# Attention inside a one-core AdaLN block: score products woven between the next head's key and query products, with two buffers for queries and keys

## The reference

```
x1  = ln(x) * (1 + scale1) + shift1
q, k, v = x1 @ qkv_w + qkv_b            # 16 heads of 128
p   = softmax(q k^T / sqrt(128))        # 128 x 128 for each sequence and head
x   = x + gate1 * ((p v) @ out_w + out_b)
x2  = ln(x) * (1 + scale2) + shift2
x   = x + gate2 * (gelu(x2 @ ffn_w1 + ffn_b1) @ ffn_w2 + ffn_b2)
out = x0 + ternary feed-forward of x (relu squared, rms norm)
```

## Time and profile before

| | us |
|---|---|
| median of 3 runs | 390.71 |
| lowest, highest | 390.7, 392.43 |
| profiled execution, span from first to last instruction | 391.2 |
| PE busy in it | 367.8 |
| DVE, ACT, POOL busy | 288.0, 237.0, 129.7 |
| mean granted PE clock | 0.980 |

### The profile page before, as it was taken

The page is one execution under the profiler, slowest core; times in us unless marked ns, Lnnn a source line. Parts: engine busy times, 40 slices in busy tenths (PEclk is TensorE's granted clock), DMA queues, the critical chain, the costliest instruction groups (busy, mean ns, idle before and its releaser), DMA issues. The chain is left out here.

```text
span 391.2 us, 6260 instructions
## 1 busy us (share of the span) xinstructions
PE 367.8 (94%) x2096; PEld 319.5 (82%) x2096; DVE 288.0 (74%) x486; ACT 237.0 (61%) x582; POOL 129.7 (33%) x111
## 2 busy tenths in 40 slices
PE   2899999999999999999999999999889899996975
PEld 2789888888888888888888898889778787885855
DVE  5775569768776976866887667689988638797793
ACT  1464576665666566656676566775687358573751
POOL 1522224321542232272323144335423300162451
PEclk9999999999999999999999999999999999998995
DMA  7913031000303100030200012010000000000002
GB/s 231 358 61 108 1 109 54 2 0 3 108 0 107 54 0 0 0 107 29 78 0 0 0 26 83 0 55 1 2 0 1 2 0 2 0 1 2 8 19 80
DMA packets 11778, 16.53 MB, mean 42 GB/s; under 512 B 672, under 2 KB 7920, under 8 KB 11760
## 3 DMA queue, kind: packets, MB, share of 16 engines
q1 hardware_dynamic: 11760, 16.30, 12.6%
HBM read 15.25 MB, written 1.05 MB: 42 GB/s over the span
## 5 line engine op out<-in xcount | busy, mean ns | idle before, releaser
L345 POOL TENSOR_TENSOR prob<-prob,rinv 128x512 f32<-128x512 f32 x32 | 33.4, 1043 | 152.4 <-DVE rinv L788 152.4
L980 PE MATMUL bank<-x_hi,wqk_hi 128*128 128x512 f32 x128 | 54.4, 425 | 0.0
L982 PE MATMUL bank<-x_hi,wqk_lo 128*128 128x512 f32 x128 | 51.3, 401 | 0.0
L981 PE MATMUL bank<-x_lo,wqk_hi 128*128 128x512 f32 x128 | 51.1, 399 | 0.0
L706 DVE TENSOR_TENSOR v_lo<-bank,v_hi 128x512 fp32r<-128x512 f32 x30 | 20.7, 691 | 39.2 <-ACT v_hi L427 39.2
L493 ACT ACTIVATE prob<-bank,nbias 128x128 f32<-128x128 f32 x128 | 45.1, 370 | 4.1 <-DVE nbias L782 4.1
L427 ACT ACTIVATE p_split<-bank 128x512 fp32r<-128x512 f32 x32 | 19.1, 598 | 35.4 <-PE bank L1014 35.4
L461 ACT ACTIVATE o_hi<-pv_pair,bias 128x512 fp32r<-128x512 f32 x31 | 21.3, 688 | 24.3 <-PE pv_pair L1029 24.3
L982 PE MATMUL bank<-k_hi,q_lo 128*128 128x128 f32 x128 | 35.4, 276 | 0.0
L417 POOL TENSOR_TENSOR raw_qk<-raw_qk 128x512 f32<-128x512 f32 x13 | 18.4, 1415 | 50.7 <-ACT raw_qk L622 50.4
L981 PE MATMUL bank<-k_lo,q_hi 128*128 128x128 f32 x128 | 35.2, 275 | 0.0
(11 more groups left out here) (206 smaller groups left out, 1086.9 us busy)
## 6 DMA issues: line engine op xcount, KB each, us to landing
raw_qk<-in_L_cond_qkv_w_dram SPq DMA_DIRECT2D x8, 512.0 KB, 4.9
raw_v<-in_L_cond_qkv_w_dram SPq DMA_DIRECT2D x4, 512.0 KB, 3.8
raw_o<-in_L_cond_out_w_dram SPq DMA_DIRECT2D x4, 512.0 KB, 3.6
xt<-in_x_dram SPq DMA_DIRECT2D x2, 512.0 KB, 5.0
xr<-in_L_cond_ada_w_dram SPq DMA_DIRECT2D x1, 1024.0 KB, 10.2
raw_w<-in_L_cond_ffn_w_dram SPq DMA_DIRECT2D x2, 512.0 KB, 7.6
t_raw<-in_L_ffn_W_fc_dram SPq DMA_DIRECT2D x4, 256.0 KB, 3.8
t_raw<-in_L_ffn_W_proj_dram SPq DMA_DIRECT2D x4, 256.0 KB, 3.9
```

The source lines that it names most:

```text
L345: nc.gpsimd.tensor_tensor(e, e, rinv[:, j % 2, :].unsqueeze(2).broadcast_to([P, SQ, P]), ALU.mult).then_inc(norm_done, 1)
L980: nc.tensor.matmul(dst, ah, bh, start=start and n == 0, stop=False)
L981: nc.tensor.matmul(dst, ah, bl, start=False, stop=False)
L982: m = nc.tensor.matmul(dst, al, bh, start=False, stop=stop and n == len(terms) - 1)
```

## The change

`scores` now takes the next unit's key and query products along. Twelve times, one 512-column matmul of the next unit's keys (the first six) or queries (the last six) is followed by one 128-column score matmul. `qk_products` remains for unit 0 alone. The wait for the previous exponentials stands ahead of the whole woven block. As the scores of unit i read q and k while those of unit i+1 are made, queries and keys alternate between two buffers; the second lies in the third and fourth part of `w2_hi` and `w2_lo`, which are therefore filled only after the attention. ACT and DVE take the keys first, then the probabilities, then the queries, and only then the exponentials and the reciprocal.

```
+        heads_q = ((q_hi[:, :], q_lo[:, :]), (w2_hi[:, w2_fourth], w2_lo[:, w2_fourth]))
+        heads_k = ((k_hi[:, :], k_lo[:, :]), (w2_hi[:, w2_third], w2_lo[:, w2_third]))
...
-        W2_AT = {2: 0, 3: 1, 6: 2, 7: 3}
+        W2_AT = {2: 0, 3: 1}
...
             def unit(G, j, vs, more, last=False):                       # ACT
                 i = UG * G + j
+                if more:
+                    biased_hi(heads_k[j1 % 2][0], ..., k_mm, i + 2, k_h)
                 if not (isinstance(i, int) and i == 0):
                     p_hi_part(i - 1)
+                if more:
+                    biased_hi(heads_q[j1 % 2][0], ..., q_mm, i + 2, q_h)
                 act.wait_ge(nb_done, i + 1)
...
-                if more:
-                    biased_hi(q_hi[:, :], bank[BQ][:, :], ...)
-                    biased_hi(k_hi[:, :], bank[BK][:, :], ...)
...
             modulate(2, SHIFT2, SCALE2, bank[0:2])
             o_hi_part(NG - 1, UG - 1)
-            w2_hi_part(3)
+            for n in range(2, 4):
+                w2_hi_part(n)
...
+            def score_step(j, n):
+                (qh, ql), (kh, kl), t = heads_q[j % 2], heads_k[j % 2], slice(n // 3 * P, (n // 3 + 1) * P)
+                m = nc.tensor.matmul(bank[BS][:, t], (ql if n % 3 == 2 else qh)[:, t], (kl if n % 3 == 1 else kh)[:, t],
+                                     start=n % 3 == 0, stop=n % 3 == 2)
...
+            def scores(G, j, more, blocks=None):
+                i = UG * G + j
+                pe.wait_ge(q_l, i + 1)
                 pe.wait_ge(k_l, i + 1)
+                if not isinstance(i, int) or i:
                     pe.wait_ge(exp_done, i)
+                if more:
+                    pe.wait_ge(wqk_l, HG * G1 + j1 % HG + 1)
+                for n in range(12):
+                    if n == 6 and blocks is not None:
+                        pe.wait_ge(v_l, blocks)
+                    if more:
+                        q_or_k_step(G1, j1, 1 - n // 6, n % 6)
+                    score_step(j, n)
...
-                scores(i, known and i == 0)
+                scores(G, j, more, blocks)
                 if not known or i >= 1:
-                    transpose_p(i - 1, (j - 1) % 2, None if blocks is None else blocks - 1)
-                if more:
-                    qk_products(*((G, j + 1) if j < UG - 1 else (G + 1, 0)))
+                    transpose_p(i - 1, (j - 1) % 2)
```

More of the change, by code:

```diff
@@ L777, in unit @@
                 first = isinstance(i, int) and i == 0
+                if not isinstance(i, int) or i >= 2:
+                    o_lo_part(*before(G, j, 2))
+                if more:
+                    G1, j1 = (G, j + 1) if j < UG - 1 else (G + 1, 0)
+                    biased_lo(heads_k[j1 % 2][1], bank[BK], HG * G1 + KB + j1 % HG, heads_k[j1 % 2][0], k_h, i + 2, k_l)
                 dve.wait_ge(s_mm, i + 1)
@@ L782, in unit @@
                 nc.vector.tensor_scalar(nbias[:, j % 2, :], negmax[:, j % 2, :], SCALE, None, ALU.mult).then_inc(nb_done, 1)
[L783 to L784 removed]
                 if not first:
                     p_lo_part(i - 1)
+                if more:
+                    biased_lo(heads_q[j1 % 2][1], bank[BQ], HG * G1 + QB + j1 % HG, heads_q[j1 % 2][0], q_h, i + 2, q_l)
                 dve.wait_ge(exp_done, i + 1)
                 nc.vector.reciprocal(rinv[:, j % 2, :], rowsum[:, j % 2, :]).then_inc(rinv_done, 1)
[L789 to L794 removed]
+                if last and j == UG - 2:
+                    add_residual(0)
                 if vs:
@@ L998, in v_block, with q_or_k_step, transpose_p @@
                                            wv_hi[:, k, :], wv_lo[:, k, :]) for k in range(KD)]).then_inc(v_mm, 1)
-            def scores(i, first):
+            def q_or_k_step(G, j, qk, n):
+                a, quad, k = j % HG, j // HG, n // 3
+                w, x, part = slice(a * P, (a + 1) * P), cols(quad), qk * KD + k
+                m = nc.tensor.matmul(bank[BK if qk else BQ][:, :], (wqk_lo if n % 3 == 2 else wqk_hi)[:, part, w],
+                                     (x_lo if n % 3 == 1 else x_hi)[:, k, x], start=n == 0, stop=n == 5)
+                if n == 5:
+                    m.then_inc(k_mm if qk else q_mm, 1)
+            def score_step(j, n):
+                (qh, ql), (kh, kl), t = heads_q[j % 2], heads_k[j % 2], slice(n // 3 * P, (n // 3 + 1) * P)
+                m = nc.tensor.matmul(bank[BS][:, t], (ql if n % 3 == 2 else qh)[:, t], (kl if n % 3 == 1 else kh)[:, t],
+                                     start=n % 3 == 0, stop=n % 3 == 2)
+                if n == 11:
+                    m.then_inc(s_mm, 1)
+            def scores(G, j, more, blocks=None):
+                i = UG * G + j
+                pe.wait_ge(q_l, i + 1)
                 pe.wait_ge(k_l, i + 1)
-                if not first:
+                if not isinstance(i, int) or i:
                     pe.wait_ge(exp_done, i)
[L1004 to L1009, removed]
+                G1, j1 = (G, j + 1) if j < UG - 1 else (G + 1, 0)
+                if more:
+                    pe.wait_ge(wqk_l, HG * G1 + j1 % HG + 1)
+                for n in range(12):
+                    if n == 6 and blocks is not None:
+                        pe.wait_ge(v_l, blocks)
+                    if more:
+                        q_or_k_step(G1, j1, 1 - n // 6, n % 6)
+                    score_step(j, n)
+            def transpose_p(i, j):
                 pe.wait_ge(norm_done, i + 1)
-                if blocks is not None:
-                    pe.wait_ge(v_l, blocks)
                 for s in range(SQ):
```

24 lines of the change are left out of this document (11 added, 13 removed).

## The result

| | before | after |
|---|---|---|
| median of 4 runs, us | 390.70 | 416.03 |
| lowest, highest | 390.65, 392.43 | 415.26, 416.39 |
| span of the profiled execution | 391.2 | 413.5 |
| its own time | not given | 415.26 |

The ratio is 1.0624, with a 95% interval of 1.059 to 1.0659: the change makes the kernel 25.3 us slower.

A forecast was written before the change was run, and what follows sets the result against it. PE was taken as the bound, never waiting in the loop, so new waits lengthen the kernel: plain units 10.7, value units 4.2, end 2.3, together 17.2 on the 391.2 us span, 408.4; median 407.9 us, range 401 to 415.

The forecast's parts named there:

- No gain from weaving: Woven block on PE: a 512-column and a 128-column product cost 0.34 us together, as before.
- The exponentials end last in plain units: Plain units: exponentials end 3.37 us after the last score product starts, so PE waits; +0.71 us each, 15 times, +10.7.
- The probabilities' low part delays value blocks: Value units: the first value block waits for DVE's low part of the probabilities; +0.30 us each, 14 times, +4.2.
- Unit 30: Its `pv` waits for DVE's residual sum, now behind the reciprocal; 10.0 us instead of 8.19, +1.8.
- Unit 0: Costed at nothing: PE goes on with value blocks not needing its softmax; up to 0.6 us if they ran short.
- rival C: DVE becomes the late one, its work exceeding its 4.2 us; some 11 units lose about 0.6 us, 414.5 us; 8%.
- The tail, "0.5 later": End of the attention: last maxima some 0.8 us late, the last reciprocal 0.5 us later; end +2.3 with unit 30.
- the late split costed at nothing: Last two parts of `w2`: 0.6 us more on ACT before the first gelu, covered by feed-forward products; uncovered 0.2.
- PE starts 0.06 after a releaser: Head of the next block in plain units: PE starts 0.06 us after the exponentials end, 3.43 instead of 3.37.
- PE waits 0.59 us: Plain units: PE is done with `pv` at 2.84 us after the last score product starts, the next block starts at 3.43.
- the things costed at nothing: Unit 0, late `w2` split, keys' low part ahead of the maxima, DMA, early wait for next weights' low part: zero.
- The median lies 0.5 lower: Step from profiled span to median time: 408.4 us on the span becomes a median of 407.9.

The follow-up runs named there:

- unweave: The changed kernel with the block in two halves, twelve key and query products and then twelve scores, same waits and buffers; 420.0 us.
- latewait: The changed kernel unwoven, with the wait for the exponentials behind the key and query products, and that for the queries' low part ahead of the sixth product; 416.04 us.
- midtrans: The changed kernel, still woven, with the transposes behind the sixth pair and the probabilities' low part ahead of the maxima on DVE; 410.45 us.
- wvlate: The changed kernel with POOL's product of `wv_lo` one unit later, in units 4, 12, 20 in place of 3, 11, 19; 413.62 us.
- before_w2late: The kernel before the change, with only the late split of the last two parts of `w2`; 391.68 us.
- best: The changed kernel unwoven, scores behind the exponentials' wait, transposes, DVE order and POOL's value weights moved, both buffers kept; 399.42 us, repeated at 398.67.
- expfirst: The changed kernel with ACT's exponentials ahead of the next queries' high part; 434.71 us.

## Why the prediction was right or wrong

**Right.** *No gain from weaving*: 0.34 us was forecast for a pair and 0.340 measured, and unweave has plain units within 0.01 us. *The exponentials end last in plain units*: forecast at T + 3.37, seen at T + 3.27, and latewait took the wait away (7.60 to 7.11 us). *The probabilities' low part delays value blocks*: +0.30 forecast, +0.36 seen, removed by midtrans. *Unit 30* waits for the residual sum, as forecast. Unit 0 cost nothing. The order of sizes (plain, then value, then end) held.

**Wrong**, by 8.1 us; 5.1 of it within the span (22.3 instead of 17.2) and 3.0 in carrying the span over to the median. The direction and the main waits were right. What failed are sizes of terms, and one term put at nothing. The largest are the baseline (3.0 us, point 6), DVE's lateness in units 4, 12 and 20 (2.0, point 1) and the tail with the late split (1.2, point 2).

1. *"In units with j = 3, 4, 7 the ternary scale or comparison stands ahead"*, kept as rival C and left out of the forecast: 2.0 us. Units 4, 12 and 20 lost 1.36 each and not 0.71. Rival C named the mechanism, but with 11 units; it holds in three, those where POOL's product falls on two small operations. wvlate shows it. I had read the 2.27 us of the earlier trace rows and asked how often DVE was late, not which of its operations lay beside which of POOL's once the phases shift.
2. *The tail, "0.5 later", and "the late split costed at nothing"*: +1.7 came, 1.2 us more. 0.9 of it is the late split: I had counted its 0.6 us on ACT and not what POOL's second low part does to DVE beside it (1.78 us instead of 0.68). before_w2late has the same rows. The remaining 0.3 I can't assign.
3. *"PE starts 0.06 after a releaser"*: it started 0.24 after ACT's end, here and in midtrans. The exponentials in turn came 0.10 early, 0.08 of it since the probabilities' high part starts at T + 0.70 and not 0.78. Together +0.08 or +0.09 in 12 units, 1.0 us. The 0.06 was the row of one wait of another place, that of `pv` for DVE's residual sum. "PE waits 0.59 us" had PE free at T + 2.84, too; it was free at T + 3.05, since `pv` waits for the probabilities' low part in plain units as well. In this kernel that lies beneath the longer wait and costs nothing.
4. *Value units "+0.30"*: +0.36, 0.8 us over 13 units. *Unit 30, "10.0 us instead of 8.19"*: 10.26, 0.3 more. Its maxima start 1.36 us behind T (295.12), where they start 0.26 behind it in unit 16, since DVE still has the output's and the keys' low part to do; the latter ahead of the maxima was among the things costed at nothing.
5. *Unit 1 as one of 14 value units*: it had no output product for cover, so its wait was 1.41 us. Inside the span this did not show, as the lower clock in the trace of before hid it.
6. *"The median lies 0.5 lower"*: I set the span of 391.2 against the median of 390.71 as if the span were a time. In every execution that gives both, the time is 1.7 to 3.0 us over the span; in the profiled one after the change it is 1.8 (415.26 and 413.5). With 1.8 for before too, my estimate, its profiled execution took about 393.0 us, 2.3 over the median, and 1.6 of that is the stretch at the lower clock in unit 1. The profiled execution after lies 0.8 below its median. 22.3 + 2.3 + 0.8 = 25.4, the difference of the medians. The spans alone say the same: the 27 executions of before beside the experiments have 388.3 to 391.3 us, the middle one 389.1, so that 391.2 stood near the top, and of the four after the change (413.5 to 414.5) the profiled one is the shortest. Had I compared unit 1 with the other value units (9.75 against 9.53, though it has six 512-column products fewer, 1.4 us), both 5 and 6 would have shown.

The chance of 8% for C, at 414.5 us, was the nearest of the four cases in time, and only a third of it was its mechanism. What the range lacked was an allowance for a baseline that is itself one execution. (Its upper bound was also added up wrongly: 391.2 + 23.8 - 0.5 is 414.5, not 414.0. The range of 401 to 415 holds either.)

What stays open: the 0.24 us of PE's restart, and the parts of best's remaining loss. A version with the old order at the start and the end and best's loop was not tried; since best's units are 0.05 to 0.08 us longer than before, I expect no gain from it.

## What to carry to other kernels

Putting short products between long ones pays only if weight loads can run ahead by more than one product; find a place in the trace where a short one follows a long one and read the step there before building it. Work that is moved ahead of its consumer takes away the cover of everything that ran beneath it (here the exponentials and two low parts), so list each wait of that stretch with its slack, and look for the units in which the usual cover does not exist. And before a span serves as baseline, compare equal stages within it: one stretch at the lower clock is worth as much as a term of the sum.

## What the runs showed of the hardware that was not expected

- Two DVE operations on 16 elements per partition took 1.21 us each beside POOL's product and 0.17 and 0.18 without it. One on 512 elements took 1.78 us beside it and 0.68 in the kernel before. Small operations lost as much as the large one.
- PE resumed 0.24 us behind the last row sum read by ACT; behind DVE's residual sum it had been 0.06. DVE's reciprocal, released by the same row sum, starts 0.04 behind it (176.47). Released by DVE, PE takes 0.06 at `pv` in the loop (175.18 to 175.24) and 0.13 at the head of the block in expfirst (176.25 to 176.38). So the loop by itself is not the reason; what is, was not tried.
- The profiled execution of before had a stretch of some 3.4 us at the lower clock while PE was busy throughout, which the same unit in before_w2late did not have. One of the two profiled executions of best had such a stretch around block 31 (granted clock 0.50 from 282.4 to 289.2 us), the other had 1.00 there; from T of unit 30 to T of unit 31 they take 9.46 and 7.98 us.
- A product's place in the order changed its own start (0.28 or 0.23 us behind a 512-column one) and never the sum.
